# One activation table placed ahead of all work on ScalarE in a decoder layer kernel

## What is computed

```python
x = _layernorm(x + _L0_attn_ref(x, Wq, Wk, Wv, Wo, bo))          # softmax over 64 keys, 16 heads of 8
x = _layernorm(x + _L0_xattn_ref(x, ctx, ctx))                   # rotated q and k, decay mask, no softmax
x = _layernorm(x + _L0_ffn_ref(x, gate, w1, w2, w3))             # top 2 of 8, silu(x w1) * (x w3) @ w2
# _layernorm: (x - mean) / sqrt(var + 1e-5)
```

## Time and profile before

| | us |
|---|---|
| median of 3 runs | 1107.57 |
| lowest and highest | 1101.7, 1109.94 |
| the profiled execution's own time | 1112.36 |
| its span, first to last instruction | 1110.5 |
| ACT busy in it | 804.6 (72%) |
| PE busy | 848.7 (76%) |
| DVE busy | 834.3 (75%) |
| POOL busy | 582.6 (52%) |

### The profile page before, as it was taken

How to read it: one execution, slowest core, us unless ns; L and a number is a source line. 1 busy time by engine, 2 the same in 40 slices (tenths; PEclk the granted TensorE clock), 3 DMA queues, 4 the chain that set the end, 5 groups by cost and what they waited for, 6 DMA issues and landing times.

```text
span 1110.5 us, 34400 instructions
## 1 busy us (share of the span) xinstructions
PE 848.7 (76%) x11844; PEld 622.8 (56%) x11844; DVE 834.3 (75%) x2039; ACT 804.6 (72%) x1672; POOL 582.6 (52%) x567
## 2 busy tenths in 40 slices
PE   3667887887887778878877666459999999999800
PEld 2455554554554545545544433249999999999700
DVE  5898887877878878788786544448888888888655
ACT  1345898888898988888889999636666666667445
POOL 0576655656766666567576622424444444444443
PEclk8777998788799987887898876569999999999955
DMA  8412212112121121111112110132222222222177
GB/s 225 128 35 40 40 25 41 31 49 41 34 50 37 44 45 33 47 36 29 43 30 47 42 35 16 42 76 66 62 59 67 62 62 64 62 63 63 39 228 230
DMA packets 136742, 68.50 MB, mean 62 GB/s; under 512 B 74528, under 2 KB 125984, under 8 KB 136576
## 3 DMA queue, kind: packets, MB, share of 16 engines
q1 hardware_dynamic: 121440, 40.56, 15.7%
q0 software_dynamic: 8640, 17.84, 4.9%
q10 hardware_dynamic: 6496, 7.89, 2.3%
HBM read 37.91 MB, written 28.34 MB: 60 GB/s over the span
## 4 chain that ended last, share of the span: by engine, by line
PE 39%; ACT 24%; issue 16%; DVE 10%; POOL 3%; DMA 1%; ACTq 1%; DVEq 1%; SPq 0%; POOLq 0%
PE QKV L780 8%; PE ST L780 8%; ACT L895 7%; PE XT L808 5%; PE SC L808 5%; PE ST L667 4%; ACT L903 3%; DVE xq_b L1240 3%; ACT ex L976 2%; ACT x L912 2%; ACT ctx_bd L941 2%; ACT q L931 2%; PE YY L581 2%; POOL frs L1614 1%; PE ST L652 1%
## 5 line engine op out<-in xcount | busy, mean ns | idle before, releaser
L1560 POOL TENSOR_TENSOR prod_ev<-e_sb,q_v 128x512 f32<-128x512 f32 x256 | 300.2, 1204 | 199.5 <-PE YY L599 165.3
L1601 POOL DMA_INDIRECT token_halves<-w_new,tok_i x142 | 135.9, 957 | 191.2 <-DVE w_new L1503 169.3
L1576 POOL DMA_INDIRECT routed_rows<-xe,pos x128 | 124.0, 969 | 102.9 <-DVE pos L1340 70.4
L1170 DVE TENSOR_TENSOR prod_qk<-q_v,QKV 128x2048 f32<-128x2048 f32 x64 | 145.6, 2276 | 0.0
L1487 DVE TENSOR_TENSOR prod_ev<-prod_qk,prod_ev 128x1024 f16<-128x1024 f32 x71 | 87.0, 1225 | 56.1 <-ACT prod_ev L1050 56.1
L1050 ACT CAST prod_ev<-prod_qk 128x1024 f16<-128x1024 f32 x71 | 74.2, 1045 | 72.6 <-DVE prod_qk L1513 55.1
L780 PE MATMUL QKV<-k_t,w_hl 128*128 128x256 f16 x852 | 117.5, 275 | 0.0
L780 PE MATMUL ST<-k_t,w_hl 128*128 128x256 f16 x852 | 117.0, 274 | 0.0
L1059 ACT ACTIVATE prod_qk<-QKV,silu_scale 128x512 f32<-128x512 f32 x142 | 96.2, 678 | 12.2 <-PE QKV L780 9.3
L1513 DVE SCALAR_TENSOR_TENSOR prod_qk<-ST,hid_scale,prod_qk 128x512 f32<-128x512 f32 x142 | 99.5, 741 | 2.8 <-ACT prod_qk L1059 1.8
L931 ACT ACTIVATE q<-XT,tab 128x256 f32<-128x256 f32 x256 | 96.6, 487 | 6.2 <-PE XT L637 6.2
(11 more groups left out here) (170 smaller groups left out, 1823.0 us busy)
## 6 DMA issues: line engine op xcount, KB each, us to landing
w_new<-routed_rows SPq DMA_DIRECT2D x71, 130.0 KB, 2.2
prod_ev<-token_halves SPq DMA_DIRECT2D x16, 512.0 KB, 5.1
x_sb<-x SPq DMA_DIRECT2D x128, 32.0 KB
head_rows<-o_n SPq DMA_DIRECT2D x128, 32.0 KB
ctx_sb<-ctx SPq DMA_DIRECT2D x32, 128.0 KB, 2.3
o_t<-head_rows SPq DMA_DIRECT2D x64, 64.0 KB, 2.5
out<-prod_qk ACTq DMA_DIRECT2D x16, 256.0 KB, 4.3
token_halves<-w_new,tok_i POOLq DMA_INDIRECT x142, 2.2
```

The source lines that it names most:

```text
L1170: eng.tensor_tensor(prod_qk[:, u, :, :].rearrange("p d (i j) -> p d i j", j=NH), q.unsqueeze(3).to_broadcast([P, HD, NH, NH]), k.unsqueeze ...
L1560: ins = eng.tensor_tensor(prod_ev[:, u, q, :, :, 0:HD], e_sb[:, it.slot(2), u, 64 * q:64 * q + 64].rearrange("p (i j) -> p j i", j=4).unsq ...
L1576: eng.indirect_dma_start(out=xs, out_offset=bass.IndirectOffsetOnAxis(ap=pos[:, r, 2 * u + k:2 * u + k + 1], axis=0), in_=xe[:, r, u, k, : ...
L1601: eng.indirect_dma_start(out=halves, out_offset=bass.IndirectOffsetOnAxis(ap=tok_i[:, s, u:u + 1], axis=0), in_=yw[:, s, u, :], in_offset= ...
```

## The change

One instruction is put at the head of ACT's program, ahead of its first wait and its first DMA: a load of function set 6, which holds the logarithm and the exponential together with Copy and Identity. Nothing else is edited. Silu, which the experts use, is not in this set.

```diff
         @block.scalar
         def _(eng):
+            eng.add_instruction(mybir.InstLoadActFuncSet(name=nc.get_next_instruction_name(), act_func_set_id=6, engine=mybir.EngineType.Activation))
             eng.wait_ge(x_in[0], 64)
             eng.dma_start(fresh(0).rearrange("p (e i) -> p e i", e=n_exp), w1.rearrange("e h i -> h e i")).then_inc(w_in[0], 16)
```

## The result

The changed kernel takes 949.27 us in the median (947.96 to 953.15, three runs) where the kernel before took 1107.57. The ratio is 0.8588, with a 95% interval from 0.8522 to 0.8653. The profiled execution took 953.15 us with a span of 951.3, so 159.2 us less than that of before. The forecast was 986 and its range ended at 955: the direction and the mechanism held, the size did not.

The account below looks back on a forecast made before the run. The prediction took ACT's table loads to set the step. Gains of 105 us in 24 full steps, 13 in the drain and 4 from other loads made 122, so 1107.6 fell to 986 us, range 955 to 1035.

Parts of the forecast that it names:

- What bounded the kernel: Full pipeline: ACT's table loads delay rs, so nb stands 2.95 us on DVE and PE waits for xq_b.
- The added load and the removed ones: ACT: one load added at the start, taken as costing nothing; 128 loads of the norms go, Silu's stays.
- The first rival: ACT: the loads stay, 129 run, and the time stays at 1108 to 1109 us; chance 0.05.
- the term of the step's length: Full pipeline: a step falls from 19.88 to 15.5 us, over 24 steps 105 us less.
- the heads' limit: The heads' way through memory, store to load to PE, allows no step under 14.5 us.
- The third rival: Full pipeline: everything fits and the step falls to 14.5 us, 146 us less in all, 962; chance 0.06.
- second rival: DVE's products stay long beside POOL's closed-up blocks and a wait remains: step 17.5 us, 1034 in all; chance 0.18.
- PE's clock: Full pipeline: the mean granted clock rises from 0.86 to over 0.90; at 1.00 PE needs 13.6 us a step.
- The fourth rival: PE: TensorE's clock falls and the kernel gets slower, 1115 us at a mean clock of 0.65; chance 0.01.
- The drain: Last five pipeline steps: gain between 0 and 5.2 us a step, middle of 2.6 taken, 13 us in all.
- the other 12 loads: Loads outside the full pipeline and drain: removing them gains at most 15.6 us, 4 taken.
- The marks I named: Signs: two loads, nb's wait gone or under 10 us, ACT near 0.76 busy, clock over 0.90, xq_b near 0.42 or 1.4.

Follow-up runs that it names:

- the last experiment: Changed kernel with SP's load of the heads put earlier and one of POOL's eight products a step moved to DVE: 968.44 us.
- the first experiment: Changed kernel with a load of the same set 6 put back ahead of every logarithm and exponential of the norms: 1109.18 us.

## Why the prediction was off, point by point

**What bounded the kernel.** Right. Loads alone bring the old time back (1.0006), and the second norm's loads bring back nb's wait and PE's wait for xq_b. One refinement: the first norm's loads cost 51 us too, by x_t and x behind them in ACT's queue.

**The added load and the removed ones.** Right: two loads are left, and the added one at 0.73 us lies in ACT's idling at the start. The first rival is out: behind the load put in by hand the trace has none until Silu. On the rule of the Trainium skill weighed there ("ScalarE activation tables: per-element evaluation and per-set limits", section "Table sets in the compiler and the runtime") the trace of after says nothing new; it was the rows of before that differed from it.

**DVE.** The wait of 67.8/24 = 2.83 us is gone in full. DVE's own work fell from 379.16 to 321.65 us, 2.40 a step: nb, xq_a and xq_b slipped through in nearly every step, and xq_b never took over 423 ns. The wait for m_sb fell from 17.3 to 4.0 us, 0.55 a step. That for sm fell from 7.9 to 1.4, 0.27. A new one for posf takes 11.3 us, 0.47. The sum is 2.83 + 2.40 + 0.55 + 0.27 − 0.47 = 5.58, which is 19.88 − 14.30; smaller waits cancel.

**The step that failed is the term of the step's length.** I had rows for 13.1 us on DVE and for 13.6 on PE, and I took 15.5: the middle between the heads' limit and a DVE with long products, and 0.3 for waits that no row showed. It measured 14.30. In 24 steps the 1.2 us are 29 of the 37 us by which the sum was short. The third rival, "all fits", to which I gave 0.06, was what happened, and the time came 13 us under even its 962. POOL's floor was left open, as 12.8 and the gaps between its issues: with them its round is 14.26 us, with the heads' 14.2 (below) the highest of the four. (The lower end of the forecast's own range, 968 for a step of 14.7, is 966 by the same sum.) I counted 0.5 us of margin ahead of POOL's start as small and as likely to shrink. In the step shown it grew to 0.6, because POOL's start is no longer set by PE's sums (345.23) but by POOL's own queue (345.92): the closed-up blocks of my second rival helped instead. The rule of the Trainium skill, "SBUF — State Buffer", section "Who interferes with whom", agrees with the runs (xq_b 418 ns where POOL waits for it, 1378 where POOL multiplies beside it), but I read it against the change, and the order in which the two engines came decided for it, as it did in the last experiment.

**The heads' limit of 14.5 us** was too high, since it took the place of the store in a step from a step in which PE's clock was in part at its lower level. The prediction's 14.78 us from the store to PE's use at 462.01 left 6.0 of slack, so 8.8 is what the way itself needs; that measured 351.68 − 342.69 = 8.99, with PE waiting at its end. The other part, from PE's L611 to the store of the same step, was 20.57 − 14.78 = 5.8 and is 14.21 − 8.99 = 5.2 where L611 comes 14.21 us after the last. Before, those 5.8 us ran at a mean granted clock of 0.82, in the columns of the earlier trace rows:

```profile
441.44:447.23 5.79, 5.79 (x111) 4.25 (x107) 4.70 (x17) 5.56 (x13) 3.85 (x5) 0.82 0.09 26
```

That the clock alone makes the difference of 0.6 us is not shown. The limit is real, as PE waits for it, but it lies 0.3 us lower.

**PE's clock.** Right in direction, and fuller than I allowed: 1.00 over the stretch, and PE's work is 326.51/24 = 13.6 us, as 0.86 × 15.8 said. The fourth rival has nothing for it.

**The drain** was the other mis-sized term: 2.6 us a step taken as the middle, 76.55/5 − 56.21/5 = 4.07 measured. Three steps of it in the changed kernel, in the columns of the earlier trace rows:

```profile
494.63:523.87 29.24, 21.18 (x276) 12.37 (x276) 20.35 (x94) 28.13 (x91) 11.94 (x13) 1.00 0.22 47
```

ACT is busy 28.13 of 29.24 us in three steps of 9.75 us. So ACT, which held the drain before, still holds these three, and PE's 7 us a step fit beside it; the gain in each, 15.31 − 9.75 = 5.56 us, is somewhat more than the four loads. The other two steps take 26.97 us with ACT busy 19.25, so something else holds them, and the mean gain is 4.07. That accounts for 7 of the 37 us; the rest of the span gave 4.8 where I took 4 for the other 12 loads.

**The marks I named.** Two loads, nb's wait gone, xq_b at 0.42, the clock over 0.90 and a wait of L611 for o_t are all as written for the case that all fits. ACT is busy 0.82 of the stretch rather than 0.76, as the step is shorter.

## What to carry to other kernels

A load of an activation table is plain time in ACT's queue, and its price is that of what waits behind it, so two functions that alternate should be given one set that has both, before anything else in the queue is tuned. When a wait is removed, ask what the instructions behind it ran beside while they were late: here their meeting with POOL was worth half of the gain with all loads in place (2.78 of 5.58 us a step) and a third with two of the four a step (27 of 86 us), and that part could be had alone by holding POOL back 3.6 us in a step where it idled 5.6. And where rows of the trace give a floor for each engine, put the forecast near the highest floor, with the gaps between a queue's issues counted in, unless a row shows what would hold it above.

## What the runs showed of the hardware that I had not expected

A load of the table that is already active takes the same 1283 ns as a switch (64 and 64 of them in the first experiment, with the time of the kernel before to 0.06%). PE's pauses went with longer work: with POOL held back and ACT's loads in place, PE's own work in 24 steps fell from 379.08 to 333.22 us while its mean granted clock rose from 0.86 to 0.99. A mean of 0.86 says that for part of that time the lower of its two levels (1.2 and 2.4 GHz) was granted. In the step of the earlier trace rows one such stretch reads, in the columns of the earlier trace rows:

```profile
457.21:464.03 6.82, 5.97 (x68) 3.89 (x56) 6.32 (x9) 4.77 (x10) 5.54 (x5) 0.50 0.01 2
```

The L611 in it takes 0.69 us, where that of the changed kernel takes 0.44. Last, where DVE and POOL multiply at once, the one that starts first keeps its length: 0.69 us on DVE beside 1.68 on POOL, or 1.66 on DVE, in the run with a product on DVE.
